# Weighted values placed ahead of the next tick's logits, a fourth buffer of exponentials, and values of 17 columns

## What is computed

```
x = x + Attention0(groupnorm(x))     # 8 heads of 16, biases by time and by particle, causal in time, softmax over 768 keys
t = t + Attention1(layernorm(t))     # additive: logits[i,j] = w2 . tanh(A[i] + B[j] + b1), 16 hidden units, softmax
t = t + Experts(layernorm(t))        # 8 experts, top 2, capacity ceil(1.25 N / 8), gelu between two products
```

## Time and profile before

| | |
|---|---|
| Runs, median (lowest to highest) | 2384.56 us (2372.84 to 2385.24), 3 runs |
| The profiled execution | 2384.78 us, span 2383.0 us |
| PE busy | 2053.2 us |
| DVE busy | 1675.7 us |
| ACT busy | 1683.2 us |
| POOL busy | 1461.3 us |
| Mean granted clock of TensorE | 0.951 of 2.4 GHz |

### The profile page before, as it was taken

How to read it: one execution, slowest core, us unless ns; L and a number is a source line. 1 busy time by engine, 2 the same in 40 slices (tenths; PEclk the granted TensorE clock), 3 DMA queues, 4 the chain that set the end, 5 groups by cost and what they waited for, 6 DMA issues and landing times.

```text
span 2383.0 us, 56242 instructions
## 1 busy us (share of the span) xinstructions
PE 2053.2 (86%) x17665; PEld 1122.5 (47%) x17665; DVE 1675.7 (70%) x4534; ACT 1683.2 (71%) x1933; POOL 1461.3 (61%) x1525
## 2 busy tenths in 40 slices
PE   2889999989998999989998999999999977549986
PEld 1344444444444444444444444444444433338775
DVE  5787787787878787868786878787877665324433
ACT  5238787877887788778787878788878977613332
POOL 3006576656666656565666666666657877627777
PEclk7799999999999999999999999999999988869998
DMA  4546322322222223222323131313131000025553
GB/s 94 89 86 128 95 48 61 55 62 56 61 56 61 56 59 57 58 60 51 66 50 68 42 70 29 81 32 77 32 65 32 12 6 4 7 54 90 84 86 37
DMA packets 157499, 137.99 MB, mean 58 GB/s; under 512 B 24665, under 2 KB 149814, under 8 KB 157104
## 3 DMA queue, kind: packets, MB, share of 16 engines
q1 hardware_dynamic: 119376, 109.87, 22.5%
q0 software_dynamic: 23824, 16.85, 5.2%
q10 hardware_dynamic: 13968, 7.30, 1.2%
HBM read 82.68 MB, written 54.52 MB: 58 GB/s over the span
## 4 chain that ended last, share of the span: by engine, by line
PE 39%; DVE 22%; issue 13%; DVEq 9%; POOL 6%; ACT 4%; POOLq 3%; DMA 2%; SPq 0%; another core or an unknown queue 0%; ACTq 0%
PE logits L978 12%; DVE max_halves L1261 4%; POOL out_dram L583 4%; PE ring L1052 3%; PE av_bank L964 3%; POOLq L802 3%; PE ring L1074 3%; PE ring L1066 3%; PE scores L948 3%; PE scores L951 2%; ACT hidden L902 2%; DVE logit_bias L1447 2%; POOL hidden L803 2%; PE ring L1071 2%; DVEq L1448 2%
## 5 line engine op out<-in xcount | busy, mean ns | idle before, releaser
L803 POOL TENSOR_SCALAR hidden<-b_rep,a_cols 128x768 f32<-128x768 f32 x1152 | 1057.1, 920 | 765.6 <-issue 302.9
L902 ACT ACTIVATE hidden<-hidden 128x2304 f32<-128x2304 f32 x384 | 816.1, 2125 | 16.4 <-POOL hidden L803 16.4
L978 PE MATMUL logits<-hidden,w_shifted 128*32 128x384 f32 x6144 | 591.6, 504 | 65.3 <-ACT hidden L906 30.9
L879 ACT ACTIVATE probs<-scores 128x512 f32<-128x512 f32 (+1 forms) x768 | 391.9, 545 | 325.6 <-PE scores L951 320.9
L1261 DVE TENSOR_REDUCE max_halves<-ring 128x1 f32<-128x384 f32 (+4 forms) x896 | 471.3, 550 | 115.8 <-PE ring L1052 114.2
L906 ACT ACTIVATE hidden<-b_rep,a_cols 128x768 f32<-128x768 f32 x384 | 358.4, 933 | 0.0
L1052 PE MATMUL ring<-k_max,q_max 112*128 112x384 bf16 (+4 forms) x1024 | 296.0, 319 | 34.8 <-DVE max_halves L1261 25.9
L978 PEld LDWEIGHTS logits<-hidden,w_shifted 128*32 128x32 f32 x6144 | 164.0, 110 | 314.9 <-issue 246.7
L948 PE MATMUL scores<-bias_q,onehot_k 112*128 112x512 bf16 (+1 forms) x768 | 276.4, 360 | 4.8 <-ACT probs L879 1.8
L951 PE MATMUL scores<-q_parts,k_parts 98*128 98x256 bf16 (+1 forms) x1536 | 277.3, 262 | 0.0
L814 POOL DMA_INDIRECT expert_rows<-rows,slots x198 | 199.5, 1007 | 64.2 <-issue 32.7
(11 more groups left out here) (262 smaller groups left out, 2585.8 us busy)
## 6 DMA issues: line engine op xcount, KB each, us to landing
qk_parts<-qk_parts_sb SPq DMA_DIRECT2D x16, 1152.0 KB, 4.7
q_parts<-qk_parts SPq DMA_DIRECT2D x192, 96.0 KB, 3.2
k_parts<-qk_parts SPq DMA_DIRECT2D x192, 96.0 KB, 4.3
q_max<-qk_parts SPq DMA_DIRECT2D x96, 96.0 KB
k_max<-qk_parts SPq DMA_DIRECT2D x96, 96.0 KB
expert_rows<-clear_row ACTq DMA_DIRECT2D x9, 792.0 KB, 5.0
x_in<-in_x_dram SPq DMA_DIRECT2D x96, 64.0 KB
x<-in_x_dram SPq DMA_DIRECT2D x96, 64.0 KB
```

Source lines behind the costliest of these rows:

```text
L803: last = g.tensor_scalar(hidden[:, q % SLOTS, o, :], b_rep[:, side], 1.0, a_cols[:, side, a_col(q, o):a_col(q, o) + 1], ALU.mult, ALU.add)
L879: s.activation(probs0[:, d % 3, 2 * pair:2 * pair + 2, 0:n_], scores[:, pair].rearrange("p (j l) -> p j l", j=2)[:, :, 0:n_], ACT.Exp) \
L902: s.activation(hidden[:, t % SLOTS, 0:3, :], hidden[:, t % SLOTS, 0:3, :], ACT.Tanh)
L978: last = mm(logits[32 * g:32 * g + 32, half, 0:HALF], w2_shifted[:, k, :], hidden[:, q % SLOTS, g, HALF * half:HALF * half + HALF], start= ...
```

## The change

Six edits. The values of a step are weighed a tick later (`VALUES_AT` 37, tick d + 13). On PE they stand at the start of slot 0, ahead of the logits, where q % 4 is not 0 and `kb` is not 0, and at the start of slot 2 otherwise, ahead of the ring uses of that slot. Of the 18 steps with `kb` other than 0, fourteen stand so in slot 0, and four (4, 8, 16, 20) are in ticks whose logits are in slot 2. `probs0` has four buffers in place of three, and ACT waits for the values of step d − 4 in place of d − 3. The values and the output tiles have 17 columns in place of 32, and DVE clears `av_bank` once at the start, since partitions 17 to 31 of each tile aren't written any more but are still copied and transposed. DVE's copy of `av_bank` moves from the start of a tick to its slot 3, behind the reads of that slot.

```
-FILL_AT, EXP_AT, VALUES_AT = 34, 35, 36
+FILL_AT, EXP_AT, VALUES_AT = 34, 35, 37
...
-        v_aug = sb("v_aug", [P, 2, TB, H, 32])
-        probs0 = sb("probs0", [P, 3, 4, QUERIES])
+        v_aug = sb("v_aug", [P, 2, TB, H, HD + 1])
+        probs0 = sb("probs0", [P, 4, 4, QUERIES])
...
-                    if positive(count := c * 24 + (d - 2)):
+                    if positive(count := c * 24 + (d - 3)):
                         act.wait_ge(av_done, count)
-                s.activation(probs0[:, d % 3, 2 * pair:2 * pair + 2, 0:n_],
+                s.activation(probs0[:, d % 4, 2 * pair:2 * pair + 2, 0:n_],
...
-                    last = mm(av_bank[32 * g:32 * g + 32, q0 - lo:q0 - lo + n_], v_aug[:, side, kb, 4 * quad + g, :],
-                              probs0[:, d % 3, g, 0:n_], start=(kb == 0), stop=(d in LAST_OF_GROUP),
+                    last = mm(av_bank[32 * g:32 * g + HD + 1, q0 - lo:q0 - lo + n_], v_aug[:, side, kb, 4 * quad + g, :],
+                              probs0[:, d % 4, g, 0:n_], start=(kb == 0), stop=(d in LAST_OF_GROUP),
...
                     for slot in range(PARTS):
+                        if ps.has(values_stage) and slot == (0 if q % 4 and STEPS[weighed][2] else 2):
+                            weigh_values(ps.batch(values_stage), ps.side(values_stage), weighed)
                         if slot == 0 and q % 4 and ps.has(stage):
                             add_logits(ps.batch(stage), q)
                         for use in parts[slot]:
...
                         if slot == 2 and q % 4 == 0 and ps.has(stage):
                             add_logits(ps.batch(stage), q)
-                        if slot == 2 and ps.has(values_stage):
-                            weigh_values(ps.batch(values_stage), ps.side(values_stage), weighed)
...
-            v.memset(v_aug[:, :, :, :, 16:17], 1.0)
+            v.memset(v_aug[:, :, :, :, HD:HD + 1], 1.0)
+            v.memset(av_bank[:], 0.0)
...
-                    stage, d = score_step(t, VALUES_AT + 1)
-                    if ps.has(stage) and d in LAST_OF_GROUP:
-                        c = ps.batch(stage)
-                        quad, lo = STEPS[d][:2]
-                        dve.wait_ge(av_done, c * 24 + (d + 1))
-                        v.tensor_copy(headsT_raw[:, quad, lo:lo + QUERIES], av_bank[:, 0:QUERIES]) \
-                         .then_inc(av_copied, 1)
+                    values_stage, weighed = score_step(t, VALUES_AT)
...
                                 read(ps, use)
+                        if slot == 3 and ps.has(values_stage) and weighed in LAST_OF_GROUP:
+                            quad, lo = STEPS[weighed][:2]
+                            dve.wait_ge(av_done, ps.batch(values_stage) * 24 + (weighed + 1))
+                            v.tensor_copy(headsT_raw[:, quad, lo:lo + QUERIES], av_bank[:, 0:QUERIES]) \
+                             .then_inc(av_copied, 1)
```

## The result

The changed kernel takes 2473.36 us (median of 4 runs, 2471.08 to 2482.55), the kernel before, run beside it, 2384.9 us. The ratio is 1.039 with a 95% interval of 1.0356 to 1.0424: 88 us slower. I forecast 2388 us in a range of 2366 to 2406.

A forecast was written before the change was run, and what follows sets the result against it. PE is busiest (86%) but holds only 39% of the chain, which alternates with DVE. Profiled 2384.8 us plus 2.9 us from PE stretches, other edits 0, gave 2388 us, no tellable change, range 2366 to 2406.

The forecast's parts named there:

- the sum of the chain: All 96 stretches of the chain on PE: 8.1 us more values, 21 trips fewer at 0.25 us, net +2.9 us.
- each stretch keeps its entry and its exit: Stated condition of the count: the chain enters and leaves each PE stretch as before, else the count fails.
- values 8 come out from under the wait for the transposes of x1 in tick 20: Ticks 21 and 22: values 8 now stand on the chain and break a join, +0.68 us in the pass.
- The round trip of 0.25 us: PE going into and out of four 32-column tiles: 0.14 in, 0.11 out; 118 trips fewer save PE 29.5 us.
- busy PE falls by some 29 us: Profile after: PE's busy time drops by this much, and its waits for DVE grow by about as much.
- what hides it is DVE itself: heads(1) in tick 7 waits for the later copy; DVE's norms and one maximum cover it: 0, otherwise some 1 us a pass.
- two halves of score fills and logits lie between on PE, 0: Values with kb = 0 wait for a copy made one to three ring uses earlier; intervening PE work covers it, 0.
- The count of stretches: Pass between 1046 and 1164 us, five PE stretches: −0.25, +0.68, −0.68, 0, +0.68, sum +0.43 us.
- Columns, fourth buffer, memset: Side edits: 17-column loads 0 (at best 8 us), fourth exponentials buffer 0, clearing av_bank at the start 0.
- Faster rival: Chain moves with PE's 29.5 us saving, DVE waiting less than 88.7 us: 2355 in full, 2370 for half; chance 0.24.
- Slower rival: heads(1)'s wait for the copy uncovered, 1 us in about 14 passes: 2402; sign: DVE waits for heads before its reciprocal; chance 0.28.
- My chances for slower were 0.28 and 0.02: 0.28: uncovered copy wait at heads(1), 2402 us; 0.02: 17-column tiles no longer run side by side, up to +500 us.

The follow-up runs named there:

- e5: Changed kernel with idle products on PE ahead of x1T(0), B(0) and heads(1), computing nothing of the result: 2415.22 us, ratio 1.0135 to the kernel before.
- e1: Changed kernel with DVE's copy of av_bank in slot 1 of its tick in place of slot 3: 2447.69 us, ratio 1.027 to the kernel before.
- g3: Kernel before, three buffers, step 18 moved to slot 2 of tick 7 and the copy of step 17 to slot 3 of tick 6; total time not given.
- g4: Kernel before, three buffers, only step 18 moved to the start of slot 2 of tick 7, copy of step 17 left early; total time not given.
- h2: Kernel before, three buffers, step 7 alone moved to the start of slot 2 of tick 20, into the wait for x1T(0): 2384.34 us, ratio 1.0015.
- e7: Kernel before with four idle products ahead of x1T(0) and five ahead of B(0), none ahead of heads(1): 2377.83 us, ratio 0.9984.
- g and h run: Kernel before, three buffers, one or a few bursts of values moved a tick later; h runs 0.9972 to 1.0015, one g run (step 8) 23 us slower.
- g1: Kernel before, three buffers, step 8 alone moved from the end of slot 2 of tick 20 to the start of slot 2 of tick 21: 23 us slower.

## Why the prediction was wrong

**The step that failed is the sum of the chain** ("2384.8 + 2.9 = 2388 us"), with its condition that "each stretch keeps its entry and its exit". It fails twice. It prices every matmul at the duration of before, and the granted clock isn't in it. The runs show 106 us more at half clock from first to last logits (run means 345 for 231, 114 us); at 0.40 to 0.46 us for each that is some 42 to 52 of the 88 us, and e5, which takes a little more than that half clock away, gives back 58. And stretches don't keep their entries: a burst that leaves a place where DVE is late leaves a wait of PE behind (0.89 us a pass in tick 8, 0.7 us more ahead of B(0)), and a late copy adds one (heads(1)). With the clock up, ticks 6 to 8 alone are 1.96 us a pass longer.

The trace of before held the warning. The mean clock of its span was 0.951, it had 48 us of half clock around logits 19, where PE waits for x1T(0) and B(0), and one of the bursts that I moved stood right in that wait. I even wrote that "values 8 come out from under the wait for the transposes of x1 in tick 20", priced it as a broken join at +0.68, and did not ask what PE does around its old place: nothing, and with the burst gone for some 2 us, twice.

**Point by point.**
- The round trip of 0.25 us: right (1.29 and 1.43 us in the chain of after). The trips are saved (122 fewer in the traces for the 118 counted); "busy PE falls by some 29 us" is wrong by 55. Matmuls at half clock take longer, and 106 us more of it is about what that needs (an estimate: half of it is 53).
- The copy of av_bank: I took 0 because "what hides it is DVE itself", and kept 1 us as a rival. The rival's price was right (0.9 in e1, 0.64 in g3), its condition too: PE's wait at L1059 changed its releaser to the copy and rose from 8.0 to 14.1 us. DVE's other work did not cover it. In e1 that wait is still 11.9 us, for the read of probsT as before, so DVE is late there for other reasons too. With the clock behind it e1 gives back 26 us.
- Values of step 18 with kb = 0, "two halves of score fills and logits lie between on PE, 0": I priced their wait and not their place, between heads(1) and attended(0), which DVE waits for. g4 has 0.71 us a pass for it, but with ACT's wait for the third buffer in it, so that the price in the changed kernel is open.
- The count of stretches, against the full clock of the table, has the right sign in three places of five: ticks 9 and 10 +0.68, measured +0.43 (logits 8 to 12); 14 and 15 −0.68, −0.42 (12 to 15); 21 and 22 +0.68, +0.57 (21 to 25); but 17 to 19 0, −0.46 (15 to 19), and 2 to 4 −0.25, +0.34 (1 to 5). The first two may be no hits either: logits 8 to 15 as a whole take 34.13 us before and 34.14 after, so a shift of logits 12 would give the same pair. That the five sum to +0.46, near my +0.43, is luck, since the single misses cancel. What lies outside, ticks 6 to 8, is +1.96, 27 us over 14 passes, and I had it at 0.
- Columns, fourth buffer, memset: 0, right (0.9991).
- Faster rival, from the 88.7 us that DVE waits for PE: refuted, they became 120.0. Slower rival: right in direction, it named one place of three and missed the clock; 2402 for 2473. Its sign, DVE waiting for heads ahead of its reciprocal, came up nine times in the window with 0.3 us each, far under the 0.65 us a pass that it needed. My chances for slower were 0.28 and 0.02.
- What the profile was to show: waits of PE for DVE did grow, by more than the 29 us, but "most of all at L1059" is wrong (+6.1; L1052 has +15.8).

**What stays open.** 34 us remain in e5 without the clock. Ticks 6 to 8 hold most of it by the table. PE's waits there grow by 1.94 us a pass: the one of tick 8 behind step 20 (0.89), the one ahead of heads(1) (0.69, of which the copy is a part), the one for the tanh (0.36). No run puts step 20 alone back, so its share is read from the traces and not tested. How the small losses at other places add up, I did not take apart. Whether a version with the joins and four buffers, but with the bursts of ticks 8, 17 and 20 left in their waits, would be faster was not tried; the h runs moved steps 1, 2, 3 and 7 alone, with three buffers.

## What to carry to other kernels

Before you move a short piece of TensorE work, ask what lies at its old place: a burst next to a wait may be what keeps the wait short and the clock up, so list the waits near 2 us and the granted clock around them before you count instructions. Putting a burst into a wait is no sure gain either (h2). Price a move twice, at full clock by the chain and at 1.2 GHz for the stretch behind each gap that it opens, and look at who waits for the engine at the new place. A test is cheap: put idle products into the gaps, and if the kernel with more work is faster and its records have less half clock, it is the clock. If it is not, the test says little, since these products cost time of their own (e7). And when you move one piece alone, move what the change gave it with it: here it was the fourth buffer, and without it ACT waits in every g and h run.

## What the runs showed of the hardware

- TensorE fell to 1.2 GHz in a kernel in which it is busy for 84% of the span, in all 12 passes behind a wait of 2.19 us with six transposes ahead of it. With waits of at most 1.48 us there, and a burst between the transposes, it held 2.4 GHz in six passes of 12. The wait alone doesn't decide: in g1 four passes held behind 2.2 us.
- Each us at half clock costs 0.46 us of the whole by e5; runs of one kernel differ by 0.40 to 0.47 us for each, in the kernel before too. That time at half clock itself varies by some 60 us between runs of one kernel (209 to 268).
- Going into and out of four 32-column tiles costs PE 0.25 us a trip in fp32, before and after alike.
- An output tile of 17 columns runs side by side with its three neighbours as one of 32 does (four matmuls start within 25 ns, and the median of one is 379 ns with both widths), and its load takes 96 ns where that of 32 columns took 109:

```profile
L964 PEld LDWEIGHTS av_bank<-probs,v_aug x3072: 92/96/120, 97.9 to 2026.7; 128*17 128x17 f32 x192
```
